# Decay exponents of second chunks from one more masked matmul, with reworked seams between the stages

## The chip, the cores and the metric

The kernel runs on one core of one Trainium2 chip. The metric is the device time of one launch in microseconds (us). The span of a profile runs from the first to the last instruction; the time of an execution is a little longer.

## The reference, cut to what matters

Four layers follow each other on 1024 tokens of width 512 (batch 4, 256 tokens each), each with a residual and a layernorm without weights:

```python
A: x = LN(x + taylor(x) + down(silu(gate(x)) * up(x)))            # hidden 1248
B: x = LN(x + down2(silu(w1'(x)) * w3'(x)))                       # hidden 1376, LoRA added to the weights
C: x = LN(x + out_proj(group_norm(ssd(conv(in_proj(x))) * silu(gate))))   # 128 heads x 64, 8 groups
D: x = LN(x + down3(silu(gate3(x)) * up3(x)))                     # hidden 2048, ternary weights
```

In C, dt is clipped, `cs` is the running sum of `dt * A` inside chunks of 128 tokens, and a sequence of 256 tokens has two chunks. For head h, source token s and target token l, inside one chunk:

```python
Lmat[l, s] = exp(cs[l] - cs[s]) if l >= s else 0
scores = (C[l] . B[s]) * Lmat[l, s]         # cb = C . B is shared by the 16 heads of a group
y[l] = sum_s scores[l, s] * x[s] * dt[s]
```

From the first chunk to the second the factor is exp(cs_second[l] + (cs_end - cs[s])). In D the weights are `sign(w) * (|w| > 0.7 * mean|w|)`, so the mean of |w| over a whole matrix comes first.

## The kernel before, in words

Tokens lie as `x_tokens` (128 partitions x 8 tiles x 512) and, turned, as `xT_hi` and `xT_lo` (a value rounded to fp32r and its rest), in two halves of 512 tokens. Products of such pairs are three matmuls, L70, L71, L72 in `three_products`.

**Stages A, B and D** are `feed_forward`: for each half `hf` a loop over hidden tiles n of 128 (10, 11 and 16 of them). TensorE does `gate_up(n)`, then `down(n-1)`; ScalarE does the SiLU and the rounded part of `hidden`; VectorE does `hidden`, and rounds (A, B) or quantises (D: L406, L410, L427, L430, in `split13` and `split2`) the weights of the tiles to come; GpSimd makes the rests of the weights in A and B and does nothing in D. `Norm` ends a half: sums (L164, or L170 and L172 in D), statistics (L182, L187), square root on ScalarE, L195 scales on VectorE, TensorE turns (L220), ScalarE and VectorE take hi and lo parts (L210, L200). For the first half this is done during the second half's first tiles, in order: in A and B before VectorE's tile 0, with TensorE waiting before `down` of tile 0; in D in tile 1. For the second half it stands at the stage's end. A stage ends with a barrier (`Stage.clear`), and the next stage's first loads are issued behind it.

**Stage C** is `state_space`. A prologue projects B and C of all groups, makes `cb` and the tables of dt and cs, and stores them to DRAM. Then 64 units (two heads each, 128 channels) run in 8 groups of 8, through `for_units`: U counts units, V = U - 1, j = U mod 2. In body(U) TensorE's order is:

```python
in_x(u, 0); squares_sum(u) if u.group_ended; in_x(u, 1)   # 24 matmuls, (16 of one column)
inside(u)                                                 # y of unit V: 32 matmuls
seg(u, 0); seg(u, 1)                                      # exponents of first chunks, h = 0, 1
in_g(u, 0); in_g(u, 1)                                    # 24
out_tile(u, 0..3)                                         # 24, out_proj of the pair before
turn(u, 0); turn(u, 1)                                    # 8 transposes
```

`seg(u, h)` (L1713 on) puts the exponents of *first* chunks of head h, mask included, into bank 6 + h: one bf16 matmul of 512 columns (L1726, identity and mask in the rows below the first 15, sums in those) and one of 56 (L1727). The exponents of *second* chunks come from VectorE: `clamp` (L1245, eight L1255 a unit) takes min(cs_second[l] - cs[s], 0). ScalarE's `decay_exp` does eight L1558 (first to second chunk), two L1563 from the banks, two L1567 over the clamped tiles. VectorE multiplies by `cb` in `decay_round` (L1243, six a unit); `cb` was masked when it was moved (`move_cb`, L1149). ScalarE's order in a unit: `x_tap` (L1437), `x_silu` (L1537), `y_high` (L1510), `decay_exp`, `gate_silu` (L1544), `gate_weights` (L1477), `square` (L1577), `y_high`. GpSimd adds the squares of a group (L1398); at a group's end TensorE's `squares_sum` (L1771) sums them over channels. The group's `rstd` scales its `group_out` into `x_tokens` (L1285).

SP's queue loads weights and rows for a unit in `load_unit`, `load_out`, `load_cs`, `load_rows` (L1087: two small DMAs) and, for a group's first unit, `load_cb`. `store_cb(g)` stores `cb` of a group in the prologue; the one of group 7 stands ahead of the first unit's loads.

Of the kernel before, what the change touches and what calls it, by code (L numbers as in the profile page):

```python
# [10 lines left out]
ALU = mybir.AluOpType  # L11
# [43 lines left out]

D_HIDDEN = 2048
# [18 lines left out]
def for_tiles(eng, tiles, body):  # L75


    body(0, 0)
    body(1, 1)
    pairs = (tiles - 2) // 2 - (0 if tiles % 2 else 1)  # L80
    pairs = pairs - 1 if tiles % 2 else pairs
    with eng.Fori(1, 1 + pairs) as i:
        body(i * 2, 0)
        body(i * 2 + 1, 1)
    for n in range(2 + 2 * pairs, tiles):
        body(n, n % 2)
# [23 lines left out]
class Shared:  # L110


    def __init__(self, nc, ctx, consts_f32):
        self.nc = nc
# [10 lines left out]
class Norm:  # L125

    def __init__(self, sh, ctx, tag, last, from_psum=True):
        nc = sh.nc  # L130
        sem = lambda n: stage_semaphore(nc, ctx, f"{tag}_{n}")
        self.sh, self.last, self.from_psum = sh, last, from_psum
# [3 lines left out]
        self.rstd = ctx.enter_context(nc.sbuf_tensor(f"{tag}_rstd", [P, HT], F32))  # L136
        self.summed = sem("summed")
# [9 lines left out]
    def vector(self, v, hf, out_done=None, scale=None):  # L147
        self.vector_sum(v, hf, out_done, scale)
        self.vector_norm(v, hf)

    def vector_sum(self, v, hf, out_done, scale):


        sh = self.sh
        for t in range(HT):
            x = sh.x[:, HT * hf + t, :]
            if self.from_psum:
                all_done, count, tile_done, before = out_done
                if t < HT - 1:
                    v.wait_ge(tile_done, before + t + 1)  # L160
                else:
                    v.wait_ge(all_done, count)
                if scale is None:
                    v.tensor_tensor(x, sh.bank[t][:, :], x, ALU.add).then_inc(self.summed, 1)  # L164
                else:

                    buf, sc, scaled = scale
                    if t >= 1 or hf:
                        v.wait_ge(self.summed, HT * hf + t)
                    v.tensor_tensor(buf, sh.bank[t][:, :], sc, ALU.mult).then_inc(scaled, 1)  # L170
                    v.wait_ge(scaled, HT * hf + t + 1)
                    v.tensor_tensor(x, buf, x, ALU.add).then_inc(self.summed, 1)  # L172

    def vector_norm(self, v, hf):

        sh = self.sh
        for t in range(HT):
            if self.from_psum:
                v.wait_ge(self.summed, HT * hf + t + 1)
            if hf and t == 0:  # L180
                v.wait_ge(self.stat, 2 * HT)
            v.bn_stats(self.stats[:, t, :], sh.x[:, HT * hf + t, :]).then_inc(self.stat, 1)  # L182
        if hf:
            v.wait_ge(self.normed, HT)
        for t in range(HT):
            v.wait_ge(self.stat, 2 * HT * hf + t + 1)
            v.bn_aggr(self.mv[:, t, :], self.stats[:, t, :]).then_inc(self.stat, 1)  # L187
        v.wait_ge(self.stat, 2 * HT * hf + 2 * HT)
        v.tensor_scalar(self.std[:, :], self.mv[:, :, 1], EPS, None, ALU.add).then_inc(self.var_ready, 1)
        v.wait_ge(self.std_ready, hf + 1)  # L190
        v.reciprocal(self.rstd[:, :], self.std[:, :]).then_inc(self.rstd_ready, 1)
        v.wait_ge(self.rstd_ready, hf + 1)
        for t in range(HT):
            x = sh.x[:, HT * hf + t, :]
            v.tensor_scalar(x, x, self.mv[:, t, 0:1], self.rstd[:, t:t + 1], ALU.subtract, ALU.mult)\  # L195
             .then_inc(self.normed, 1)
        if not self.last:
            for k in range(KT):
                v.wait_ge(self.x_hi, KT * hf + k + 1)
                v.tensor_tensor(sh.xl[:, k, HALF * hf:HALF * (hf + 1)], sh.bank[k][:, :],  # L200
                                f32(sh.xh[:, k, HALF * hf:HALF * (hf + 1)]), ALU.subtract)\
                 .then_inc(self.x_ready, 1)

    def scalar(self, a, hf):
        a.wait_ge(self.var_ready, hf + 1)
        a.activation(self.std[:, :], self.std[:, :], ACT.Sqrt).then_inc(self.std_ready, 1)
        if not self.last:
            for k in range(KT):
                a.wait_ge(self.turned, KT * hf + k + 1)
                a.activation(self.sh.xh[:, k, HALF * hf:HALF * (hf + 1)], self.sh.bank[k][:, :], ACT.Copy)\  # L210
                 .then_inc(self.x_hi, 1)

    def tensor(self, pe, hf):

        if self.last:
            return
        pe.wait_ge(self.normed, HT * (hf + 1))
        for k in range(KT):
            for t in range(HT):
                mm = pe.transpose(self.sh.bank[k][:, P * t:P * (t + 1)],  # L220
                                  self.sh.x[:, HT * hf + t, P * k:P * (k + 1)], self.sh.ident[:, :])
            mm.then_inc(self.turned, 1)


def feed_forward(nc, sh, kind, w13_dram, w2_dram, tiles, extra, out_dram=None):
# [3 lines left out]
    TL = tiles  # L229
    with Stage(nc) as ctx:  # L230
# [6 lines left out]
        norm = Norm(sh, ctx, kind, kind == "D")  # L237

        if kind == "B":
            raw13 = sb("raw13", [P, TL, 2 * D])  # L240
            raw2 = sb("raw2", [P, TL, D])
        else:
            raw13 = sb("raw13", [P, 2, 2 * D])
            raw2 = sb("raw2", [P, 2, D])
        w13h = sb("w13h", [P, 2, 2 * D], F32R)
# [8 lines left out]
        raw13_in = [sem(f"raw13_in{i}") for i in range(2)]  # L254
        raw2_in = [sem(f"raw2_in{i}") for i in range(2)]
        w13_hi, w13_ready = sem("w13_hi"), sem("w13_ready")
# [5 lines left out]
        extra_in = sem("extra_in")  # L262
# [44 lines left out]
        if kind == "D":  # L307
            scales = sb("scales", [P, 2, TL])
            down_scale = sb("down_scale", [P, D])
            ones = sb("ones", [P, P])  # L310
            thr, nthr = sb("thr", [P, 4]), sb("nthr", [P, 4])
            above = sb("above", [P, 2 * D])
            above2 = sb("above2", [P, D])
            scaled_out = sb("scaled_out", [P, D])
            total_mm, thr_done = sem("total_mm"), sem("thr_done")
            above_done, above2_done, scaled = sem("above_done"), sem("above2_done"), sem("scaled")
            ones_set = sem("ones_set")
# [4 lines left out]
        def _(sp):  # L322
# [23 lines left out]
            if kind == "D":  # L346
                sp.dma_start(scales[:, :, :], extra["scales"]).then_inc(extra_in, 16)
                sp.dma_start(down_scale[:, :], extra["down_scale"]).then_inc(extra_in, 16)
            free13 = w13_ready
            free2 = w2_ready  # L350
            for hf in range(2):
                def load(n, par):
                    slot = (hf * TL + par) % 2
                    if hf or not isinstance(n, int) or n >= 2:
# [10 lines left out]
            if kind == "D":  # L365
                for hf in range(2):
                    sp.wait_ge(norm.normed, HT * (hf + 1))
# [21 lines left out]

        @block.vector  # L390
        def _(v):
            scale = (scaled_out[:, :], down_scale[:, :], scaled) if kind == "D" else None
# [57 lines left out]
            def hidden(hf, n, par):  # L450
# [11 lines left out]
                else:  # L462
                    v.tensor_tensor(hid[:, slot, :], up, gated[:, slot, :], ALU.mult).then_inc(hid_done, 1)
                if hf or not isinstance(n, int) or n >= 2:
# [36 lines left out]
            if kind == "D":  # L501
                v.memset(ones[:, :], 1.0).then_inc(ones_set, 1)
                v.wait_ge(total_mm, 1)
                v.tensor_scalar(thr[:, 0:3], sh.bank[0][:, 0:3], 1.0 / (D * D_HIDDEN), THRESHOLD, ALU.mult, ALU.mult)\
                 .then_inc(thr_done, 1)
                v.wait_ge(thr_done, 1)
                v.tensor_scalar(nthr[:, 0:3], thr[:, 0:3], -1.0, None, ALU.mult).then_inc(thr_done, 1)
                v.wait_ge(thr_done, 2)
# [9 lines left out]
            else:  # L518
                split13(0, 0, 0)
# [15 lines left out]
            for hf in range(2):  # L535
# [17 lines left out]
                if hf and kind != "D":  # L553
                    norm.vector(v, 0, (down_mm, TL, rows_done, 0), scale)
                elif hf:
                    norm.vector_sum(v, 0, (down_mm, TL, rows_done, 0), scale)

                def body(n, par):
                    if not (isinstance(n, int) and n + 2 >= TL):
# [8 lines left out]
                    hidden(hf, n, par)  # L568
# [27 lines left out]
                    if kind == "D" and hf and isinstance(n, int) and n == 1:  # L596
                        norm.vector_norm(v, 0)
# [1312 lines left out]
```

## Time and profile before

| | us |
|---|---|
| median of 3 runs | 2311.48 (2309.84 to 2311.51) |
| the profiled execution: time | 2312.29 |
| the profiled execution: span | 2310.5 |
| TensorE busy | 2132.7, mean granted clock 0.958 |
| VectorE busy | 1762.6 |
| ScalarE busy | 1214.7 |
| GpSimd busy | 673.3 |

Stages by the time line: A to 269, B to 517, C's prologue to 649, C's units to 2040, C's end to 2091, D to the end. Busy time of TensorE counts modelled ends of pipelined matmuls; the distance between two starts tells more.

### The profile page before, as it was taken

To read this page: it belongs to the slowest core of one execution; us is meant where nothing else is said; L and a number is where in the kernel's file an instruction comes from. 1 tells how busy PE (TensorE), PEld (TensorE's weight loads), DVE (VectorE), ACT (ScalarE), POOL (GpSimd) and SP (SyncE) were. 2 spreads that over 40 slices of the span, in tenths; PEclk is the share of its full clock that TensorE was granted. 3 is DMA by queue.
4 is the path that set the end of the run, shared out by engine and by line. 5 is a ranking of instruction groups with operands and counts; after the bars stand their busy time and mean duration, and the time that the engine had idled before them with its cause. 6 is when DMAs were issued, how large, how long until landed. Compare 5 with 4: busy or idle time off the path is not lost. (4 is left out here: it accounts for less than half of the span.)

```text
span 2310.5 us, 36141 instructions
## 1 busy us (share of the span) xinstructions
PE 2132.7 (92%) x10769; PEld 1700.1 (74%) x10833; DVE 1762.6 (76%) x2970; ACT 1214.7 (53%) x2182; POOL 673.3 (29%) x406
## 2 busy tenths in 40 slices
PE   7999589988979999999999999999999999967997
PEld 6777478767867777777777777777777777755775
DVE  6434355547868888889889889889889889867887
ACT  2112113334347677667667767767767767732232
POOL 5525044321113324324324324324324324310000
PEclk9999789999989999999999999999999999978998
DMA  4202231213232212212212212212212212103433
GB/s 156 96 28 73 83 133 62 89 47 98 92 106 70 69 60 70 69 60 69 69 60 69 69 60 69 69 60 69 69 60 68 69 61 69 51 0 123 137 109 109
DMA packets 126014, 176.30 MB, mean 76 GB/s; under 512 B 17668, under 2 KB 83716, under 8 KB 125316
## 3 DMA queue, kind: packets, MB, share of 16 engines
q1 hardware_dynamic: 125892, 175.07, 23.8%
q14 instruction: 93, 0.76, 0.1%
q8 instruction: 29, 0.48, 0.1%
HBM read 165.72 MB, written 9.31 MB: 76 GB/s over the span
## 5 line engine op out<-in xcount | busy, mean ns | idle before, releaser
L70 PE MATMUL bank<-xT_hi,C_w_hi 128*128 128x512 f32 x1160 | 478.3, 412 | 14.1 <-POOL C_w_lo L1380 7.5
L72 PE MATMUL bank<-xT_hi,C_w_lo 128*128 128x512 f32 x1160 | 464.9, 401 | 0.0
L71 PE MATMUL bank<-xT_lo,C_w_hi 128*128 128x512 f32 x1160 | 464.6, 401 | 0.0
L1380 POOL TENSOR_TENSOR C_w_lo<-C_raw,C_w_hi 128x512 fp32r<-128x512 f32 x130 | 186.7, 1436 | 736.5 <-ACT C_w_hi L1477 640.3
L1127 DVE SCALAR_TENSOR_TENSOR C_acc<-bank,C_par,C_acc 128x510 f32<-128x510 f32 (+2 forms) x384 | 281.2, 744 | 70.3 <-ACT C_acc L1437 44.8
L1243 DVE TENSOR_TENSOR C_decay<-C_decay,C_cb 128x512 f32<-128x512 f32 x384 | 299.1, 807 | 4.5 <-ACT C_decay L1563 4.5
L70 PEld LDWEIGHTS bank<-xT_hi,C_w_hi 128*128 128x128 f32 x1160 | 222.1, 191 | 70.5 <-POOL C_w_lo L1380 8.8
L72 PEld LDWEIGHTS bank<-xT_hi,C_w_lo 128*128 128x128 f32 x1160 | 221.9, 191 | 54.2
L71 PEld LDWEIGHTS bank<-xT_lo,C_w_hi 128*128 128x128 f32 x1160 | 222.9, 192 | 47.6
L1398 POOL TENSOR_TENSOR C_sq_sum<-C_sq_sum,C_sg 128x1024 f32<-128x1024 f32 x56 | 154.3, 2756 | 212.8 <-DVE C_decay L1243 121.5
L70 PE MATMUL bank<-C_out_hi,C_yg_hi 128*128 128x512 f32 x512 | 202.0, 395 | 7.8 <-DVE C_yg_lo L1213 5.5
L72 PE MATMUL bank<-C_out_hi,C_yg_lo 128*128 128x512 f32 x512 | 201.1, 393 | 0.0
L71 PE MATMUL bank<-C_out_lo,C_yg_hi 128*128 128x512 f32 x512 | 200.0, 391 | 0.0
L1224 DVE TENSOR_TENSOR C_group_out<-bank,C_group_out 128x512 f32<-128x512 f32 x192 | 131.0, 687 | 81.9 <-PE bank L72 81.9
L1437 ACT ACTIVATE C_acc<-bank,C_par_two 128x512 f32<-128x512 f32 x128 | 98.5, 775 | 151.8 <-PE bank L72 144.4
L1706 PE MATMUL bank<-C_decay,C_xd 128*64 128x256 f32 x1024 | 159.2, 390 | 4.3 <-DVE C_decay L1243 4.3
L1558 ACT ACTIVATE C_decay<-C_cs_second,C_end_t 128x128 f32<-128x128 f32 x512 | 157.1, 389 | 0.8
L1537 ACT ACTIVATE C_xs<-C_acc 128x512 f32<-128x512 f32 x128 | 80.5, 629 | 140.6 <-DVE C_acc L1127 140.5
L1510 ACT ACTIVATE C_yg_hi<-C_xs,C_par_two 128x512 fp32r<-128x512 f32 x128 | 92.5, 722 | 90.3 <-DVE C_xs L1208 56.5
L70 PEld LDWEIGHTS bank<-C_out_hi,C_yg_hi 128*128 128x128 f32 x512 | 96.4, 188 | 32.1 <-issue 11.7
L1213 DVE SCALAR_TENSOR_TENSOR C_yg_lo<-C_xs,C_par,C_yg_hi 128x512 fp32r<-128x512 f32 x128 | 113.3, 885 | 3.5 <-ACT C_yg_hi L1510 3.4
L72 PEld LDWEIGHTS bank<-C_out_hi,C_yg_lo 128*128 128x128 f32 x512 | 96.5, 189 | 21.3
(245 smaller groups left out, 4399.3 us busy)
## 6 DMA issues: line engine op xcount, KB each, us to landing
C_raw<-in_Cxg SPq DMA_DIRECT2D x65, 512.0 KB, 3.6
C_cs_second<-cs_rows SPq DMA_DIRECT2D x64, 512.0 KB, 5.0
C_raw_out<-in_Cout SPq DMA_DIRECT2D x64, 256.0 KB, 3.5
D_raw<-in_D SPq DMA_DIRECT2D x32, 512.0 KB, 3.5
A_raw<-in_A SPq DMA_DIRECT2D x20, 512.0 KB, 3.6
B_right_raw<-in_D SPq DMA_DIRECT2D x16, 512.0 KB, 3.7
D_raw<-in_D SPq DMA_DIRECT2D x32, 256.0 KB, 2.6
cb_rows<-C_decay SPq DMA_DIRECT2D x8, 768.0 KB, 3.3
```

What stands on the lines that cost most here:

```text
L70: pe.matmul(out, lh, rh, start=start, stop=False)
L71: pe.matmul(out, lh, rl, start=False, stop=False)
L72: return pe.matmul(out, ll, rh, start=False, stop=stop)
L1127: v.scalar_tensor_tensor(out=sums[:, :, i:], in0=src[:, :].rearrange("p (b t) -> p b t", b=2)[:, :, 0:SEQ - i], scalar=w(TAPS - 1 - i), in ...
L1213: v.scalar_tensor_tensor(out=yg_lo[:, slot, half(h)], in0=xs[:, slot, half(h)], scalar=par_of(V, NORM_W), in1=f32(yg_hi[:, slot, half(h)]) ...
L1224: v.tensor_tensor(group_out[:, t, :], bank[OUT_BANK[k % 4]][:, :], group_out[:, t, :], ALU.add)\
L1243: v.tensor_tensor(e, e, cb[:, r % 2 if r < 4 else 2, :], ALU.mult).then_inc(S.m_done, 1)
L1380: e.tensor_tensor(w_lo[:, slot, :], raw_at, f32(w_hi[:, slot, :]), ALU.subtract).then_inc(lo_done, 1)
L1398: e.tensor_tensor(sq_sum[:, :], sq_sum[:, :], sg[:, 1 - u.j, :], ALU.add).then_inc(S.sq_added, 1)
L1437: a.activation(sums[:, half(h)], src[:, :], ACT.Identity, scale=scale, bias=bias).then_inc(done, 1)
L1558: a.activation(decay[:, 2 * h + b // 2, SEQ * (b % 2) + CHUNK:SEQ * (b % 2 + 1)], cs_second[:, u.j, at:at + CHUNK], ACT.Exp, bias=end_t[:, ...
L1706: pe.matmul(bank[4 + th][q, at:at + SEQ], xd[:, 2 * b, q], decay[:, 2 * h + th, at:at + SEQ], start=True, stop=False)
```

## The change

**In C's units.** `clamp` and its table `cs_t` go, and so do the two L1567 on ScalarE. The sums of both chunks are split into three bf16 parts and stored (`chunk_rows`). `seg(u, c)` now handles chunk c for both heads; `seg(u, 0)` stands where both calls stood, `seg(u, 1)` behind `in_g` and ahead of `out_tile`. Both chunks use banks 6 and 7, so `seg(u, 1)` waits for ScalarE's two exponentials over the first chunks' exponents, and ScalarE's order is `inside_exp(u, 0)`, `across_exp(u)`, `inside_exp(u, 1)`. As masks lie in the matmuls, `move_cb` only copies: 3 operations for 5. `load_rows` has four DMAs for two. In a group's first unit `square` stands ahead of `gate_silu`. In the prologue two of five `dt_turn` go, the parts are made over 1024 columns for 512, and `store_cb(7)` stands behind the first unit's `load_rows`.

**At C's end.** The first two weight tiles of D are loaded, D's threshold is made and its first tile quantised while C's last output tiles run, which get banks of their own. Only the first half of the tokens is normalised there, two of its four scalings on ScalarE; the second half is only summed.

**In A, B and D.** The norm of a half that runs under the next half's tiles is spread over tiles 0 to 3: statistics in tile 0, reciprocal and scaling (all four on ScalarE) in tile 1, the turning in tiles 2 and 3, two blocks each, into the banks of the tile before, with TensorE waiting for the hi and lo parts behind `down`. In D the second half of C's tokens is treated so in the first pass. D's `hidden` stands ahead of its weight work, its rest part is made by GpSimd (`hidden_low`), and so are the residual sums (`half_add`). At a stage's end two of four scalings move to ScalarE. `for_tiles` writes out four first tiles for two.

```diff
-            def seg(u, h):
-                if h == 0:
-                    pe.wait_ge(S.rows_in, u.U * 32 + 32)
...
+            def seg(u, c):
+                if c == 0:
+                    pe.wait_ge(S.rows_in, u.U * 64 + 64)
...
+                for h in range(2):
+                    if c:
+                        pe.wait_ge(S.decays, u.U * EXPS + (h + 1))
+                    elif not u.first:
+                        pe.wait_ge(S.xd_done, u.V * 2 + (h + 1))
+                    pe.matmul(bank[6 + h][:, :], left[:, c, h, :], right[:, c, h, :], start=True, stop=False)
+                    pe.matmul(bank[6 + h][:, :].rearrange("p (b l) -> p b l", b=BATCH)[:, :, 0:REST], left_rest[:, :],
+                              right_rest[:, :, :], start=False, stop=True).then_inc(S.seg_mm, 1)
...
                 seg(u, 0)
-                seg(u, 1)
                 in_g(u, 0)
                 in_g(u, 1)
+                seg(u, 1)
...
-                decay_exp(u)
+                inside_exp(u, 0)
+                across_exp(u)
+                inside_exp(u, 1)
+                if u.group_ends:
+                    square(u)
                 gate_silu(u, 0)
                 gate_silu(u, 1)
...
-                clamp(u, 0)
-                clamp(u, 1)
                 out = not u.first_pair
...
                 load_cs(u)
                 load_rows(u)
+                if u.first:
+                    store_cb(GROUPS - 1)
...
+                    turns = nm is not None and n in (2, 3)
+                    if turns:
+                        pe.wait_ge(hid_done, n + hf * TL)
+                        for k in (2 * n - 4, 2 * n - 3):
+                            nm.turn(pe, k, turn_bank(hf, n, k))
...
                         down(hf, n - 1, 1 - par, isinstance(n, int) and n == 1, False)
+                    if turns:
+                        pe.wait_ge(nm.x_ready, 2 * n - 2)
...
+            def norm_steps(hf, n):        # vector
+                nm = in_pass[hf]
...
+                if n == 0:
+                    for t in range(HT):
+                        nm.stats_of(v, t, nm is not early)
+                    nm.spread(v)
+                elif n == 1:
+                    nm.invert(v)
+                elif n < 4 and not (kind == "D" and hf):
+                    for k in (2 * n - 4, 2 * n - 3):
+                        nm.low(v, k, turn_bank(hf, n, k))
...
+            def norm_steps(hf, n):        # scalar
...
+                if n == 0:
+                    nm.root(a)
+                elif n == 1:
+                    for t in range(HT):
+                        nm.scale_shift(a, t)
+                elif n < 4 and not (kind == "D" and hf):
+                    for k in (2 * n - 4, 2 * n - 3):
+                        nm.high(a, k, turn_bank(hf, n, k))
...
+            first_quantised()             # vector, end of C
+            mean_square(last, GROUPS)
             group_scale(GROUPS)
...
+            for k in range(HT):
+                last_add(k)
+                if k:
+                    norm.stats_of(v, k - 1)
+            norm.stats_of(v, HT - 1)
+            norm.spread(v)
+            norm.invert(v)
+            for t in range(HT // 2):
+                norm.scale(v, t)
+            for k in range(HT, TT):
+                last_add(k)
+            for k in range(KT):
+                norm.low(v, k, bank[TAIL_BANK[k]])
```

## Rows read from the trace of the kernel before

**Rows 1.** The page, section 1: busy us, share of the span, instructions.
```profile
PE 2132.7 (92%) x10769; PEld 1700.1 (74%) x10833; DVE 1762.6 (76%) x2970; ACT 1214.7 (53%) x2182; POOL 673.3 (29%) x406
```

**Rows 2.** Stretches: length, busy us of PE, PEld, DVE, ACT, POOL, clock, DMA.
```profile
1460.00:1480.97 20.97, 20.81 (x118) 16.49 (x117) 17.69 (x32) 15.50 (x28) 6.23 (x4) 1.00 0.09 26
1020.86:1024.27 3.41, 3.41 (x10) 2.64 (x9) 1.97 (x4) 0.00 (x0) 0.00 (x0) 0.50 0.73 249
2120.00:2180.00 60.00, 60.00 (x259) 48.41 (x258) 50.84 (x88) 13.39 (x22) 0.00 (x0) 1.00 0.44 146
```

**Rows 3.** Time line of TensorE, unit 39, around seg: start, length.
```profile
1501.65 0.19 PE L1727 MATMUL bank<-C_right_rest,C_left_rest 128*128 128x56 bf16 x1 [0.16 <-issue]
1501.68 0.38 PE L1726 MATMUL bank<-C_right,C_left 128*128 128x512 bf16 x1
1501.89 0.19 PE L1727 MATMUL bank<-C_right_rest,C_left_rest 128*128 128x56 bf16 x1
1501.92 0.48 PE L70 MATMUL bank<-xT_hi,C_w_hi 128*128 128x512 f32 x1
1502.24 0.39 PE L71 MATMUL bank<-xT_lo,C_w_hi 128*128 128x512 f32 x1
```

**Rows 4.** Groups by line: count, busy and mean, idle before them.
```profile
L1255 DVE TENSOR_SCALAR C_decay<-C_cs_second,C_cs_t 128x128 f32<-128x128 f32 x512 | 106.1, 280 | 2.6 <-DMA C_cs_second<-cs_rows 2.6
L1405 POOL TENSOR_TENSOR x_tokens<-C_group_out,x_tokens 128x512 f32<-128x512 f32 x28 | 35.5, 1301 | 0.0
```

**Rows 5.** Time line, unit 39: ScalarE's exponentials, TensorE's first output matmul.
```profile
1504.33 1.28 ACT L1558 ACT_TABLE_LOAD   x1
1505.63 2.45 ACT L1558 ACTIVATE C_decay<-C_cs_second,C_end_t 128x128 f32<-128x128 f32 x8
1507.60 0.39 PE L70 MATMUL bank<-C_out_hi,C_yg_hi 128*128 128x512 f32 x1
1507.98 1.05 ACT L1563 ACTIVATE C_decay<-bank 128x512 f32<-128x512 f32 x2
```

**Rows 6.** Time line around a group's end, units 16 and 17.
```profile
1006.24 1.28 ACT L1558 ACT_TABLE_LOAD   x1
1007.75 0.49 PE L70 MATMUL bank<-C_out_hi,C_yg_hi 128*128 128x512 f32 x1 [1.11 <-DVE C_yg_lo L1213]
1016.01 2.37 POOL L1398 TENSOR_TENSOR C_sq_sum<-C_sq_sum,C_sg 128x1024 f32<-128x1024 f32 x1 [13.12 <-ACT C_sg L1577]
1016.81 2.12 DVE L1243 TENSOR_TENSOR C_decay<-C_decay,C_cb 128x512 f32<-128x512 f32 x1
1018.51 1.94 PE L1771 MATMUL bank<-C_ones,C_sq_sum 128*128 128x1 f32 x16 [1.35 <-POOL C_sq_sum L1398]
```

**Rows 7.** Time line, unit 19: ScalarE's exp table, TensorE's first output matmul.
```profile
1074.60 1.28 ACT L1558 ACT_TABLE_LOAD   x1
1075.69 0.39 PE L70 MATMUL bank<-C_out_hi,C_yg_hi 128*128 128x512 f32 x1
```

**Rows 8.** Waits of TensorE: us in total, times, longest.
```profile
PE bank L220 <- DVE x_tokens L195: 32.6, 4, 11.0
PE bank L787 <- DVE D_hidl L467: 9.6, 5, 4.7
PE bank L1727 <- DMA C_right<-first_rows: 8.9, 1, 8.9
PE bank L70 <- DVE A_hidl L467: 5.6, 1, 5.6
```

**Rows 9.** Time line, end of C to the start of D.
```profile
2077.93 2.73 DVE L1285 SCALAR_TENSOR_TENSOR x_tokens<-C_group_out,C_rstd,x_tokens 128x512 f32<-128x512 f32 x4
2089.65 1.31 DVE L200 TENSOR_TENSOR xT_lo<-bank,xT_hi 128x512 fp32r<-128x512 f32 x2 [0.16 <-ACT xT_hi L210]
2099.38 0.77 PE L771 MATMUL bank<-xT_hi,D_w13h 128*128 128x512 f32 x1 [6.39 <-DVE D_w13h L410]
```

**Rows 10.** Groups by line of VectorE, 2110 to 2180 us (stage D).
```profile
L467 DVE TENSOR_TENSOR D_hidl<-D_hid,D_hidh 128x512 fp32r<-128x512 f32 x12 | 8.3, 692 | 9.1 <-ACT D_hidh L694 9.1
```

More of the change, by code:

```diff
@@ L75, in for_tiles @@
 def for_tiles(eng, tiles, body):
[L78 to L82, printed above, removed]
+    for n in range(4):
+        body(n, n % 2)
+    pairs = (tiles - 4) // 2 - 1
+    with eng.Fori(2, 2 + pairs) as i:
         body(i * 2, 0)
         body(i * 2 + 1, 1)
-    for n in range(2 + 2 * pairs, tiles):
+    for n in range(4 + 2 * pairs, tiles):
         body(n, n % 2)
@@ L113, in __init__ @@
     def __init__(self, nc, ctx, consts_f32):
[L114 removed]
+        self.nc, self.ctx = nc, ctx
+        self.ahead = None
         self.x = ctx.enter_context(nc.sbuf_tensor("x_tokens", [P, TT, D], F32))
@@ L174, in vector_norm @@
-    def vector_norm(self, v, hf):
-        sh = self.sh
-        for t in range(HT):
[L178 to L222, printed above, removed]
+    def x(self, t):
+        return self.sh.x[:, HT * self.hf + t, :]
@@ L235, in sem @@
             return stage_semaphore(nc, ctx, f"{kind}_{name}")
-        norm = Norm(sh, ctx, kind, kind == "D")
+        norms = [HalfNorm(sh, ctx, f"{kind}{hf}", hf) for hf in range(2)]
+        early = HalfNorm(sh, ctx, f"{kind}_in", 1) if kind == "D" else None
+        in_pass = (early, norms[0])
         if kind == "B":
@@ L746, in body @@
                              .then_inc(term_hi, 1)
-                    if kind == "D" and hf and isinstance(n, int) and n == 1:
-                        norm.scalar(a, 0)
-                if hf and kind != "D":
-                    norm.scalar(a, 0)
+                    norm_steps(hf, n)
                 for_tiles(a, TL, body)
-            norm.scalar(a, 1)
+            norms[1].root(a)
+            for t in range(HT // 2, HT):
+                norms[1].scale_shift(a, t)
+            if kind != "D":
+                for k in range(KT):
+                    norms[1].high(a, k, sh.bank[k])
         @block.tensor
@@ L881, in _ @@
                 down(hf, TL - 1, (TL - 1) % 2, False, True)
-            norm.tensor(pe, 1)
+            if kind != "D":
+                for k in range(KT):
+                    norms[1].turn(pe, k, sh.bank[k])
 PAR = 8
@@ L979, in state_space @@
         rstd = sb("rstd", [P, TT])
-        raw_bc = sb("raw_bc", [P, 2, BC])
+        raw_bc = ahead.first
         consts_raw = sb("consts_raw", [P, P + HALF])
@@ L1376, in _ @@
+            for k in range(KT):
+                norm.low(v, k, bank[TAIL_BANK[k]])
         @block.gpsimd
@@ L1617, in _ @@
             root(GROUPS)
-            for hf in range(2):
-                norm.scalar(a, hf)
+            group_scaled(last, GROUPS)
+            norm.root(a)
+            for t in range(HT // 2, HT):
+                norm.scale_shift(a, t)
+            for k in range(KT):
+                norm.high(a, k, bank[TAIL_BANK[k]])
         @block.tensor
@@ L1793, in _ @@
             inside(last)
-            for k in range(TT):
-                out_tile(last, k)
-            squares_sum(last)
-            pe.wait_ge(S.ms_done, GROUPS)
-            for hf in range(2):
-                if hf:
-                    pe.wait_ge(norm.x_ready, KT)
-                norm.tensor(pe, hf)
+            pe.wait_ge(S.g_silu, last.U * 2)
+            pe.matmul(bank[3][:, 0:3], ahead.ones[:, :], sh.abs_totals[:, :], start=True, stop=True).then_inc(S.total_mm, 1)
+            out_tile(last, 0)
+            out_tile(last, 1)
+            squares_sum(last)
+            for k in range(2, TT):
+                out_tile(last, k)
+            for k in range(KT):
+                norm.turn(pe, k, bank[TAIL_BANK[k]])
 DT_V = 10
```

431 lines of the change are left out of this document (260 added, 171 removed).

## The prediction

> **What bounds the kernel now.** I read the page first: TensorE is busy 92% of the span, VectorE 76% [rows 1]. Then the stretches. A regular unit of stage C takes 20.97 us, and TensorE is busy in 20.81 of them at full clock, VectorE in 17.69, ScalarE in 15.50 [rows 2]. Sixty-four units are 1,370 of the 2,310 us, so what counts there is TensorE's order alone: every matmul added to it is paid, and work taken from VectorE is worth nothing by itself. D's loop is the same: 60.00 of 60 us [rows 2]. Third, the waits of TensorE [rows 8] and the time lines around them: its idle time lies at the seams, at the turn from one half of the tokens to the other, and once a group. Behind such idle time the clock falls to its lower level: in the 3.41 us behind a group's end it was 0.50, so a fall costs 1.7 us beside the idle time [rows 2, 6]. The sum below is made against the profiled execution, 2312.3 us (span 2310.5); the median is 2311.5, so 0.8 comes off at the end.
>
> **1. The second seg, every unit.** Two matmuls of 512 columns and two of 56 join TensorE's order. From one L1727 to the next, over one L1726, are 0.24 us, so four take 0.48; the first L70 behind them lasts 0.32 to the next start where 0.23 is usual, 0.09 more [rows 3]. That is 0.57 us. Before the first L1727 the trace also shows 0.16 us of "issue"; it comes after `inside`, whose last matmuls are short, and I don't expect it behind `in_g`. Bounds 0.48 to 0.73; 64 x 0.57 = **+36 us** (31 to 47). No other work hides it, TensorE is full. The removed `clamp`, 106.1 us of VectorE [rows 4], and the L1567 return nothing: VectorE waits for the output matmuls next anyway.
>
> **2. A new wait in TensorE's order.** `seg(u, 1)` waits for ScalarE's exponentials over the first chunks, since banks 6 and 7 are theirs; behind it stand the output matmuls and all that follows. In unit 39 the table is loaded by 1505.6 and two exponentials take 1.05, to 1506.7; TensorE is through with `in_g` at 1507.6: 0.9 us to spare [rows 5]. Units with j = 0 have a margin 1.0 shorter, so some 0.4 for the first head, none for the second. In a group's first unit the table is there at 1007.5, the exponentials end 1008.1 and 1008.6, while `in_g` ended 1.11 + before 1007.75 [rows 6]: output begins at about 1009.0 instead of 1007.75, 0.7 beyond the 0.57. In the units behind a group's end ScalarE is late by `root` and `group_scaled`: in unit 19 its exponentials could end at 1076.4, TensorE wants them at 1075.7 [rows 7]. I add 0.7 + 0.6 + 0.2 + 0.3 us for the first four units of a group, each stall giving the next unit slack: 1.8 x 7 = **+12 us**. Below: nothing but the first, 4. Above: if ScalarE's chain follows TensorE in all j = 0 units, 0.5 more each, 25.
>
> **3. A group's end.** The sum of squares kept TensorE waiting 1.35 us at 1018.5 [rows 6]. ScalarE's `square` moves ahead of a table load, two SiLUs and a copy (1.28 + 1.1 + 0.6): GpSimd begins some 3 us earlier relative to ScalarE, and the wait goes: 7 x 1.3 = **-9 us**. What becomes late next is VectorE: the GpSimd addition now falls on `decay_round`, which waits behind it as at 1016.81 (2.12 us for one) [rows 6]; the next unit needs its products 5 us later, so this is hidden. The sixteen one-column matmuls, 1.9 us, stay, so the clock may still fall. I take half of 7 x 1.7: **-6 us** (0 to -12).
>
> **4. C's start.** The rows of the first unit stood behind `store_cb(7)` in SP's queue and TensorE waited 8.9 us [rows 8]. Now they go ahead. What is late next is `move_cb(7)`, three copies behind the last `cb` matmul, about 2.3 us. 8.9 - 2.3, and less time at the lower clock, but second `seg` needs exponentials that wait for the store: **-7 us** (-3 to -11). The prologue's fewer transposes (-1) and longer parts on VectorE (+1) cancel.
>
> **5. From C to D.** Before, the last sum of the second half starts at 2077.93, its norm and turning end at 2090.96, and D's first matmul is at 2099.38 behind a barrier, a load and the quantising [rows 9]. After: output tiles end at 2062 as before; `group_add`, `last_add` and statistics of the first half until 2065.9, scaled by 2068, turned and split by 2073; barrier 1.5; D starts at **2074.5**, 24.9 earlier. But the second half's norm is now in D's first tiles. VectorE has statistics (3 us) in tile 0; ScalarE waits for them with the root, loads tables twice (1.28 each) and has the SiLU of tile 1 behind it; so tile 1's `hidden` comes at +16 us, the reciprocal at +22, four scalings to +24.4, while TensorE wants to turn at +14.8. Then `low` stands behind `split2(n+1)`, which waits for the very `down(n-1)` that precedes TensorE's wait: 2.5 and 3.6 us more. With 5 us at the lower clock tile 4 starts at about +44, where +23 was usual. 24.9 - 21.5: **-3 us** (-20 if the steps fit under the matmuls, +6).
>
> **6. The half turns of A and B.** The waits of 5.6 us [rows 8] and 3.4 at the lower clock go. In their place: 2.6 for the scalings (again behind the root and its tables), and twice about 2 for `split2` and two `low` behind `down`. With the clock: **0** (-9 to +7 for both). Ends of A and B: two of four scalings beside the others, 0.5 each: **-1**.
>
> **7. D.** Its half turn cost waits of 2.7, 0.8 and 4.7 (of the 9.6 in [rows 8]) and two falls. Spread out, statistics and both table loads still stand between tile 0 and the `hidden` of tile 1: about 8 us and one fall: **-4** (-10 to +2). The end: GpSimd adds while VectorE multiplies, -2.1, and `hidl` 0.6 longer: **-1.5**. The loop: VectorE has 50.84 us in 60 [rows 2], 10.8 tiles of 24 matmuls, 4.7 a tile of 5.56. `hidl` (0.69 [rows 10]) goes to GpSimd (1.30 [rows 4]): **+1** (0 to +10).
>
> The memory rule behind that last bound: the Trainium skill, "SBUF — State Buffer", section "Who interferes with whom", says that GpSimd and a VectorE instruction with two SBUF inputs exclude each other for a whole instruction. By that rule the trace agrees at 1016.81 [rows 6].
>
> A rule that speaks against moving roots into tile 0: the Trainium skill, "ScalarE: Activation LUTs", section "What ACT_TABLE_LOAD costs", gives 2.66 us for a switch, a drain of 1.38 included. The row says otherwise: the load starts 1504.33, takes 1.28, and the exponential starts 1505.63 [rows 5]. By the page the three half turns and D's start would each be 2.8 us worse; I go by the row.
>
> **Sum.** 36 + 12 - 9 - 6 - 7 - 3 + 0 - 1 - 4 - 1.5 + 1 = +17.5. 2312.3 + 17.5 - 0.8 = **2329 us**.
>
> **Rivals.**
> - *TensorE paced by ScalarE* (10 in 100): the new wait bites in all j = 0 units. Part 2 at 25 instead of 12, clock falls at each group's end stay, +6: 2348. For it: the margin of 0.4. Against it: TensorE's unit grows by 0.57, and ScalarE's by nothing.
> - *The seams fit* (other side, 22 in 100): the spread norm costs TensorE only the structural waits of some 2 us, because scaling ends before tile 2's `gate_up`. Then part 5 gives -20, part 6 -8, part 7 another -6: 31 less, 2298; from 22 less on the kernel is faster. For it: VectorE is idle for about half of each tile in A and B. Against it: the in-order queue of ScalarE, where SiLU(1) stands behind the root.
> - *Half of that* (10 in 100): 18 less, 2311, no change.
> - *D held by VectorE* (8 in 100): each GpSimd `hidl` blocks VectorE for 1.30 us; 4.7 - 0.69 + 1.30 = 5.3 is still under 5.56, but GpSimd's own instruction stretches to 1.7 when both meet, and VectorE's waits with it: 5.9, +0.35 x 28 tiles = +10: 2339. The page on SBUF named above is the general form of this.
> - *The change doesn't do what it says*: the second `seg` costs nothing, since its operands are bf16 and short. Only if TensorE had gaps; 20.81 of 20.97 excludes it. None.
> - The forecast, 50 in 100; its own range 2316 to 2342.
>
> **Chances and range.** A measurement can't tell less than 0.2%, 4.6 us, from no change. Faster: the fitting seams, 22, less a few where parts 1 and 2 are at their tops: 0.20. Same: 0.13. Slower: 0.67. The bounds of the loop (35 to 72) and the seams (-41 to +10) don't fall together; I keep 2300 to 2347, which leaves the best seams and the worst pacing out.
>
> **What would show it.** Regular unit 21.5 us in the stretches, with L1726 128 more times; a wait of TensorE for ScalarE's L1563 successor before some seg; no wait of L1771 for GpSimd; D's first matmul some 25 us before its old place relative to C's last output tile; in tiles 1 to 3 behind each turn, waits of transposes for ScalarE's scalings and of gate_up for VectorE's `low`. It is wrong if the unit grows by over 0.9 or under 0.4, or if those waits are absent.

## The result, and the profile after

The changed kernel takes 2348.7 us (median of 4 runs, 2348.6 to 2351.2) against 2311.5 (2309.8 to 2314.8): ratio 1.0164, 95% interval 1.0151 to 1.0176, 37 us slower. The forecast was 2329: the direction came, at twice the size, and the time lies 1.7 us above the range.

First the changed kernel's page and stretches. The columns are those of [rows 2]: length, then busy us of PE, PEld, DVE, ACT, POOL, granted clock and DMA.

```profile
PE 2161.6 (92%) x11017; PEld 1710.1 (73%) x11081; DVE 1700.0 (72%) x2383; ACT 1226.8 (52%) x2207; POOL 741.8 (32%) x450
...
1482.00:1503.50 21.50, 21.34 (x121) 16.70 (x121) 16.79 (x25) 15.40 (x28) 5.81 (x4) 1.00 0.17 50
...
1032.70:1035.70 3.00, 3.00 (x14) 2.13 (x13) 2.85 (x6) 0.00 (x0) 0.00 (x0) 1.00 0.95 302
166.80:173.70 6.90, 5.71 (x18) 4.89 (x19) 1.98 (x2) 3.12 (x6) 6.74 (x6) 0.51 0.24 97
...
2117.08:2175.44 58.36, 42.39 (x152) 33.38 (x153) 35.55 (x59) 16.72 (x24) 9.10 (x5) 0.78 0.23 78
```

A regular unit now takes 21.50 us. The 3.00 us behind the sum of squares at a group's end run at clock 1.00, where the same work ran at 0.50 before [rows 2]. A's half turn (166.8) runs at 0.51, the lower of the two levels (1.2 GHz). The last row is D's start, from its first `gate_up` to that of the seventh tile (five whole tiles and the sixth's `gate_up`), called D's first five tiles below: 58.4 us with TensorE busy in 42.4. Here is the same work before:

```profile
2099.38:2133.68 34.30, 33.53 (x137) 26.72 (x138) 27.85 (x49) 8.16 (x12) 0.00 (x0) 0.95 0.42 132
```

TensorE's waits after: total, times, longest, to be read beside [rows 8]. L1853 and L1854 are `seg`, L1830 is `inside`, L192 the turning, L72 and L851 the matmuls that need `xT_lo` (`low`, L201), L867 `down`.

```profile
PE bank L192 <- ACT x_tokens L186: 34.4, 6, 9.4
...
PE bank L1853 <- ACT C_decay L1671: 15.4, 14, 1.4
PE bank L1830 <- issue: 13.0, 7, 1.9
...
PE bank L72 <- DVE xT_lo L201: 9.2, 4, 3.0
...
PE bank L867 <- POOL D_hidl L654: 8.4, 4, 5.1
...
PE bank L851 <- DVE xT_lo L201: 6.6, 2, 4.0
```

The waits for the sum of squares (8.9 before) and for the first unit's rows (8.9) are gone. New are `seg`'s (forecast), seven of 1.86 us ahead of `inside` (not forecast; the profile names no releaser, "issue"), and those for `low`.

The two time lines, laid over each other by the starts of TensorE's matmuls, say where the 36.6 us of span came from. The middle column is the forecast for the same stretch, from its own terms.

| stretch | forecast | measured |
|---|---|---|
| A and B, to C's first matmul (521.90, now 529.03) | -1 | +7.1 |
| C's prologue, to the first unit | 0 | +1.0 |
| first unit, to its first turning | -6 | -5.3 |
| units, first turning to last (1358.75, now 1398.95) | +32 | +40.2 |
| last turning to D's first matmul (64.53, now 39.26) | -24.9 | -25.3 |
| D (211.12, now 230.02) | +17.4 | +18.9 |

Four of the six rows fit to 1.5 us or better. The miss is in A and B (8 us) and in the units (8 us). In the units, 63 steps from one to the next grew by 0.52 each, 33 us; the first step grew 2 us beyond that (its cause was not followed up) and the groups' ends 5.

The time line around a group's end, unit 17, TensorE and then VectorE (start, length; in brackets the idle time before):

```profile
1020.99 0.39 PE L1853 MATMUL bank<-C_right,C_left 128*128 128x512 bf16 x1 [1.43 <-ACT C_decay L1671]
...
1035.31 0.39 PE L74 MATMUL bank<-xT_hi,C_w_lo 128*128 128x512 f32 x1
1037.56 0.65 PE L1830 MATMUL bank<-C_decay,C_xd 128*64 128x256 f32 x4 [1.86 <-issue]
```

```profile
1025.99 2.88 DVE L1332 TENSOR_TENSOR C_decay<-C_decay,C_cb 128x512 f32<-128x512 f32 x1
...
1034.76 2.51 DVE L1221 SCALAR_TENSOR_TENSOR C_acc<-bank,C_par,C_acc 128x510 f32<-128x510 f32 x3
1037.19 0.16 DVE L1346 TENSOR_SCALAR C_ms<-bank 128x8 f32<-128x8 f32 x1
```

`inside` starts 0.2 us after L1346, `mean_square`, has ended. That operation reads the sums out of bank 4, which `inside` overwrites, and stands behind three convolutions in VectorE's order. The wait's cause can be read from this coincidence, but only the runs below show it.

D's second and third tile, ScalarE, then what TensorE and VectorE do at their end:

```profile
2125.06 1.28 ACT L168 ACT_TABLE_LOAD   x1
2131.62 0.21 ACT L168 ACTIVATE D_in_std<-D_in_std 128x4 f32<-128x4 f32 x1 [5.27 <-DVE D_in_std L164]
2131.84 1.28 ACT L749 ACT_TABLE_LOAD   x1
2133.14 0.69 ACT L749 ACTIVATE D_gated<-bank,ahead_scales 128x512 f32<-128x512 f32 x1
...
2139.23 2.92 ACT L186 ACTIVATE x_tokens<-x_tokens,D_in_shift,D_in_rstd 128x512 f32<-128x512 f32 x4 [3.96 <-DVE D_in_shift L174]
```

```profile
2147.77 0.75 DVE L471 SCALAR_TENSOR_TENSOR D_w2h<-ahead_raw,ahead_nthr,D_above 128x512 fp32r<-128x512 f32 x1
2148.44 1.28 DVE L201 TENSOR_TENSOR xT_lo<-bank,xT_hi 128x512 fp32r<-128x512 f32 x2
```

ScalarE waits 5.27 us for the statistics with the SiLU of the next tile behind the root; the scalings end at 2142.15 and TensorE, which had waited 9.37 us for them, turns at 2142.30. At the end of the tile `low` (L201) runs behind `split2` (L471), and the next `gate_up` starts at 2149.78, 0.06 after it.

### The profile page after: what moved, and what is told of

It is laid out like the page before. It is cut to its first block and busy times, and to the rows that moved or that the text cites. A ratio compares the mean times of both kernels' runs of the same rounds, so it can differ in the third digit from the quotient of the medians.

```text
span 2347.1 us, 35872 instructions
## 1 busy us (share of the span) xinstructions
PE 2161.6 (92%) x11017; PEld 1710.1 (73%) x11081; DVE 1700.0 (72%) x2383; ACT 1226.8 (52%) x2207; POOL 741.8 (32%) x450
## 5 line engine op out<-in xcount | busy, mean ns | idle before, releaser
L72 PE MATMUL bank<-xT_hi,C_w_hi 128*128 128x512 f32 x1160 | 473.3, 408 | 16.2 <-POOL C_w_lo L1493 9.0
L73 PE MATMUL bank<-xT_lo,C_w_hi 128*128 128x512 f32 x1160 | 459.8, 396 | 0.0
L74 PE MATMUL bank<-xT_hi,C_w_lo 128*128 128x512 f32 x1160 | 459.7, 396 | 0.0
L1493 POOL TENSOR_TENSOR C_w_lo<-C_raw,C_w_hi 128x512 fp32r<-128x512 f32 x130 | 180.1, 1385 | 717.3 <-ACT C_w_hi L1591 639.7
L1332 DVE TENSOR_TENSOR C_decay<-C_decay,C_cb 128x512 f32<-128x512 f32 x384 | 336.6, 904 | 8.9 <-ACT C_decay L1680 8.9
L72 PEld LDWEIGHTS bank<-xT_hi,C_w_hi 128*128 128x128 f32 x1160 | 220.3, 190 | 70.4 <-POOL C_w_lo L1493 10.3
L1313 DVE TENSOR_TENSOR C_group_out<-bank,C_group_out 128x512 f32<-128x512 f32 x184 | 126.1, 685 | 177.3 <-PE bank L74 177.3
L72 PE MATMUL bank<-C_out_hi,C_yg_hi 128*128 128x512 f32 x512 | 205.4, 401 | 2.0 <-issue 2.0
L1830 PE MATMUL bank<-C_decay,C_xd 128*64 128x256 f32 x1024 | 159.7, 389 | 17.3 <-issue 13.0
L1671 ACT ACTIVATE C_decay<-bank 128x512 f32<-128x512 f32 x256 | 137.6, 590 | 0.7
L1302 DVE SCALAR_TENSOR_TENSOR C_yg_lo<-C_xs,C_par,C_yg_hi 128x512 fp32r<-128x512 f32 x128 | 121.6, 950 | 5.4 <-issue 3.1
L72 PEld LDWEIGHTS bank<-C_out_hi,C_yg_hi 128*128 128x128 f32 x512 | 96.5, 188 | 27.6 <-issue 2.0
```

The lines of the kernel that those rows point to most:

```text
L72: pe.matmul(out, lh, rh, start=start, stop=False)
L73: pe.matmul(out, lh, rl, start=False, stop=False)
L74: return pe.matmul(out, ll, rh, start=False, stop=stop)
L1302: v.scalar_tensor_tensor(out=yg_lo[:, slot, half(h)], in0=xs[:, slot, half(h)], scalar=par_of(V, NORM_W), in1=f32(yg_hi[:, slot, half(h)]) ...
L1313: v.tensor_tensor(group_out[:, t, :], bank[OUT_BANK[k % 4]][:, :], group_out[:, t, :], ALU.add)\
L1332: v.tensor_tensor(e, e, cb[:, r % 2 if r < 4 else 2, :], ALU.mult).then_inc(S.m_done, 1)
```

## Experiments

Twelve kernels. Ratios are to the kernel before, run on the same chip, with 95% intervals; "from the change" is the difference to 2348.7.

**1. The old loop in the changed seams.**

```diff
-                seg(u, 0); in_g(u, 0); in_g(u, 1); seg(u, 1)      # TensorE, per unit
+                seg(u, 0); seg(u, 1); in_g(u, 0); in_g(u, 1)      # one chunk, head h
+                clamp(u, 0); clamp(u, 1)                          # VectorE, and masks in move_cb again
```

> The changed kernel with the loop over the units as before: one seg, the clamps on VectorE, the mask in the cb products. All seams stay changed. Reading of the changed trace: a regular unit went from 20.98 to 21.50 us, 64 x 0.52 = 33.7, and at a group's end the second seg waits 1.43 + 0.90 us for ScalarE where 1.11 was waited before, 7 x 1.2 = 8.5; so 2348.7 - 42 = 2306. Rival, that the waits are there in any case and only move: 2348.7 - 33.7 = 2315. Rival, that the changed seams gain nothing and the loop costs all of the difference: 2311.

Measured: 2307.1 us, 0.9975 (0.9966 to 0.9985), 41.6 below the change. So the loop costs 42 us and all the changed seams together are worth 5. A regular unit is 20.93 us here and 21.51 in the changed kernel, 0.58 for the loop alone. The wait at `inside` is there in this kernel too (15.1 us in seven times): it belongs to the seam, not to the second `seg`. Four of the seven are 2.4 us long, and behind three of these four the clock fell; those groups' second units take 26.6 to 26.9 us where three of the others take 24.6. The first of the three falls:

```profile
1199.95:1203.36 3.41, 3.41 (x24) 2.64 (x20) 2.52 (x4) 2.23 (x4) 0.00 (x0) 0.50 0.00 0
```

**2. `mean_square` ahead of the convolutions.**

```diff
+                if u.group_ended:
+                    mean_square(u, g)
                 for h in range(2):
                     ... tap, three conv ...
-                    if u.group_ended and h == 0:
-                        mean_square(u, g)
```

> The changed kernel with VectorE's mean_square ahead of the first half's convolutions in a group's second unit. If the 1.86 us before inside (seven times, called issue) are the wait for mean_square behind three convolutions, they go: 2348.7 - 13 = 2336. Rival: inside waits as long for the masked decays or the scaled x, which VectorE also makes late there: 2348. Rival: the wait goes, but the next unit's second seg waits longer for ScalarE, whose root is behind the same mean_square: half, 2342.

Measured: 2333.6 us, 1.0091 (1.0074 to 1.0108), 15.1 below. The wait of L1830 for "issue" is gone from the list, a group's second unit falls from 25.24 to 23.34 us in all seven groups (13.3 in sum), and the next unit's 22.8 stays. It was `mean_square`.

**3. A's and B's half turn as before.**

```diff
-        in_pass = (early, norms[0])
+        in_pass = (early, norms[0] if kind == "D" else None)
+        # VectorE, ahead of the second pass: stats, spread, invert, scale x4, low x4
+        # TensorE, ahead of the first down: turn x4
```

> The changed kernel with the half turns of A and B in one go as before (all four scalings on VectorE ahead of the second pass, the turning before the first down). By the stretches of the two traces A's turn took 57.8 us where 51.2 were before, B's 51.3 where 48.5 were: 2348.7 - 9.4 = 2339. Rival, the forecast's part 6, that the turns cost the same and A and B are longer for another reason (their ends): 2348.

Measured: 2338.8 us, 1.0114 (1.0097 to 1.0131), 9.9 below. C's first matmul comes 10.0 us earlier than in the changed kernel, so the half turns carry the whole difference of A and B (7.1).

**4. The second `seg` between the output tiles.**

```diff
-                seg(u, 1)
                 for k in range(HT):
+                    if k == 2:
+                        seg(u, 1)
                     out_tile(u, k)
```

> The changed kernel with the second seg between the second and the third output tile instead of ahead of the first. If the wait of TensorE for ScalarE's first exponentials is all that the place costs, the units with excess (1.83 and 1.30 us beyond a regular unit in each group) fall to the 0.75 that the output matmuls wait for yg_lo anyway: 7 x (1.1 + 1.3) = 17, 2332. Rival, that what TensorE gains there it gives back at inside behind a group's end, since VectorE's chain and its mean_square don't come earlier: 7 x 1.3 = 9, 2340. Rival, that the exponentials over the second chunks, now 2.8 us later, hold the turning of x: 64 x 0.3 slower, 2360 and over.

Measured: 2337.9 us, 1.0114 (1.0097 to 1.0131), 10.9 below, between the first two. But for 0.5 us in the very first pair, `seg` doesn't wait for ScalarE any more; a group's first unit falls from 23.33 to 22.38 and its third from 22.82 to 21.53, but the second, with the wait at `inside`, goes from 25.24 to 25.39, and to 27.1 in the two groups where the clock falls behind it. Part of the gain is given back there.

```profile
PE bank L1830 <- issue: 13.9, 7, 2.0
```

The third theory is out: the exponentials over the second chunks, 2.8 us later, hold nothing; a regular unit is 21.53.

**5. The norm's steps one tile later** (root in tile 1, scalings in 2, turning in 3 and 4).

```diff
-        STATS, ROOT, INVERT, SCALE, TURN = 0, 0, 1, 1, 2
+        STATS, ROOT, INVERT, SCALE, TURN = 0, 1, 2, 2, 3      # `for_tiles` writes out six first tiles for four
```

> The changed kernel with the steps of the spread norm one tile later in A, B and D: root behind hidden of tile 1, reciprocal and scalings at the end of tile 2, turning in tiles 3 and 4. If what costs is that root stands ahead of the SiLU of tile 1 in ScalarE's order while VectorE's statistics are not there, TensorE's waits of 10.9 us in A, 6.7 in B and 16 in D and their clock falls go in large part: -6, -5 and -20, 2318. Rival, that the steps cost their own time on ScalarE and VectorE wherever they stand: the waits move by a tile and the time stays, 2347.

Measured: 2333.7 us, 1.0092 (1.0075 to 1.0108), 15.0 below, half of the first theory. TensorE's waits for scalings fall from 34.4 to 21.5 us, and those for `low` stay (9.4 + 7.6 where 9.2 + 6.6 were). So the place of the steps is one cause of two. That it is the root ahead of the SiLU is read from the time line above and not shown by itself: this run moves the root, the scalings and the turning together.

**6. `low` ahead of `split2`.**

```diff
+                    norm_lows(hf, n)                  # tiles 2 and 3 behind a turn
                     split2(hf, n + 1, 1 - par)
                     ...
-                    for k in (2 * n - 4, 2 * n - 3):  # was at the tile's end
-                        nm.low(v, k, turn_bank(hf, n, k))
```

> The changed kernel with the two low of tiles 2 and 3 behind a turn ahead of split2 in VectorE's order, where they wait for the turning only and not for the down that follows it. The waits of gate_up for low are 3.03 + 2.06 us in A, 1.79 + 2.35 in B and 2.62 + 3.98 in D, 15.8 in all, and part of the lower clock is behind them. If the order on VectorE causes them: 2348.7 - 14 - 3 = 2332. Rival, that ScalarE's high is what is late (behind silu and hidden of the same tile): two thirds stay, 2344.

Measured: 2332.9 us, 1.0097 (1.0080 to 1.0114), 15.8 below. The waits for `low` fall by 6.4 us only:

```profile
PE bank L72 <- DVE xT_lo L201: 5.7, 3, 2.3
...
PE bank L855 <- DVE xT_lo L201: 3.7, 2, 2.8
```

By the starts of `gate_up`, though, A's turn is 7.0 us shorter, B's 3.3 and D's first five tiles 7.8, 18 in sum. The rest goes with time at the lower clock: 129 us of the profile are at the lower level where 160 were. Both theories had a part: what remains is `high` and `low` one after the other, what went was `split2` and the clock behind it.

**7. All of it together.** The edits of runs 1, 2, 5 and 6 in one kernel.

> The loop as before, mean_square ahead of the convolutions, the norm's steps one tile later, and low ahead of split2, in one kernel. If the parts add up: 2348.7 - 41.6 (old loop) - 15.1 (mean_square) - 15.0 (steps later) - 17 (low first) = 2260. Rival, that they overlap, since with the old loop the waits of a group's end were partly for GpSimd's sum and the low waits are fewer when the steps are later: 2275. Against the kernel before: 0.978 to 0.985.

Measured: 2261.5 us, 0.9784 (0.9767 to 0.9800). The parts add up to 87.5, and 87.3 came. This agreement is in part luck, for by stretches they don't add up: the units, first turning to last, are 57.9 us shorter where the four runs' own differences make 50.8 (run 1 still had the wait at `inside` and its three falls), and all the rest of the span is 30 us shorter where they make 42, as runs 5 and 6 shorten the same turns.

**8. Both halves normalised at C's end.**

```diff
-        early = HalfNorm(sh, ctx, f"{kind}_in", 1) if kind == "D" else None
+        early = None
+            norm2 ... stats, spread, invert, scale, turn, high, low behind norm's, at C's end
```

> The changed kernel with the norm of the second half of tokens at C's end, behind that of the first, instead of in D's first tiles. The norm in D's tiles costs 58.4 us over five tiles where 34.3 were before, 24.1 more; at C's end it should cost a root, scalings, transposes, high and low behind the first half's, 9 to 13 us. So 2348.7 - 24 + 11 = 2336. Rival, that most of the stretch in D's first tiles is the lower clock and the first tile's own start and stays: 2352.

Measured: 2333.5 us, 1.0099 (1.0082 to 1.0116), 15.3 below. D's first five tiles are regular again, 25.1 us less, with D starting 9.3 us later behind C's last unit:

```profile
2125.23:2158.48 33.25, 33.25 (x137) 26.61 (x138) 29.82 (x45) 9.21 (x13) 9.16 (x5) 0.95 0.42 138
```

**9 and 10. The best seams, with the old loop and with the changed one.** Run 9 adds the edit of run 8 to run 7. Run 10 has run 9's seams, the changed loop and run 4's place for the second `seg`.

> The kernel with the old loop, mean_square first, steps one tile later and low first, and the norm of both halves at C's end, so that D's first tiles are regular. In that kernel D's first five tiles take 49.8 us; with both norms at C's end they took 33.2, and C's end grew by 8.2: 2261.5 - 16.6 + 8.2 = 2253, against the kernel before 0.975. Rival, that the gain at D's start and the better order there are the same gain, 2260.

> The same seams with the changed loop (second seg, between the second and third output tile). If what the second seg costs is its own matmuls alone once its wait is gone: 34 above its sister with the old loop, 2287. Rival, that its waits at a group's end stay as well: 42 above, 2295.

Measured: 2255.0 us, 0.9755 (0.9739 to 0.9771), 6.4 less than run 7 of the 8.4 expected, and 2283.4 us, 0.9883 (0.9866 to 0.9900). With its waits gone the changed loop costs 28.4 us, less than both theories. Regular units differ by 0.60 us (21.53 and 20.93), 38 in all, and a group's first and third unit give some of it back: the output matmuls' wait for `C_yg_lo` is 1.0 us there where run 9 has 9.8. That this is because `clamp` is no longer in VectorE's way was not tested.

**11 and 12. The kernel before with `square` moved, and with `mean_square` moved too.**

```diff
                 decay_exp(u)
+                if u.group_ends:
+                    square(u)
                 gate_silu(u, 0)
```

> The kernel before with one edit: in a group's first unit square stands right behind the exponentials in ScalarE's order. By part 3 of the forecast the wait for the sum of squares goes and the clock falls half as often: 2311.5 - 15 = 2296. By the changed trace TensorE then waits for mean_square at inside, 1.86 us of the 1.35 + 1.7 gained: 7 x 1.2 = 8 or, as the group's period in the changed seams with the old loop says (173.8 us where it was 173.9), next to nothing: 2304 to 2311.

> The kernel before with square moved as in the run beside it, and mean_square ahead of the first half's convolutions. If mean_square behind three convolutions is what took the gain back, the whole of it comes out here: 7 x 2.9 = 20, 2291. Rival, that inside then waits for the masked decays instead: 2304 or above.

Measured: 2310.5 us, 1.0000 (0.9991 to 1.0010), and 2295.4 us, 0.9932 (0.9915 to 0.9948). The move alone can't be told from nothing (the units of its trace are 4.3 us shorter); with `mean_square` out of the convolutions' way it is worth 17 us by the medians, and 15.9 in the units of the trace. `mean_square` moved alone in this kernel was not run. Run 11's time line, TensorE and VectorE:

```profile
1022.43 0.39 PE L72 MATMUL bank<-xT_hi,C_w_lo 128*128 128x512 f32 x1
1024.52 0.65 PE L1709 MATMUL bank<-C_decay,C_xd 128*64 128x256 f32 x4 [1.71 <-issue]
```

```profile
1021.73 2.51 DVE L1127 SCALAR_TENSOR_TENSOR C_acc<-bank,C_par,C_acc 128x510 f32<-128x510 f32 x3
1024.15 0.16 DVE L1271 TENSOR_SCALAR C_ms<-bank 128x8 f32<-128x8 f32 x1
```

`inside` again starts when `mean_square` is through (1024.31). In this kernel nothing else of the change is present, so the step is isolated.

## Why the prediction was wrong, step by step

**Part 1, the second seg: right.** 0.52 us a unit for 0.57, 33.5 for 36, and against run 1, which differs in the loop alone, 0.58. That nothing of VectorE's relief comes back held for regular units; at a group's end run 10 gets some 1.4 us back each, which may be that relief.

**Part 2, the wait for ScalarE: right in size and nearly in place.** The forecast spread it over a group's first four units; it came in two. The 15.4 us are 1.43 in a group's first unit (six times), 0.90 in its third (seven) and 0.50 in the very first; 0.23 between the heads comes to 3 more, and the 5.5 us that the output matmuls waited for `C_yg_lo` (one is in [rows 6]) went in exchange. Net 13 for 12; run 4 gave 10.9 for undoing it. The rival, TensorE paced by ScalarE in all units with j = 0, is out: 14 waits in 64 units. The measured time is the 2348 of that rival by coincidence only.

**Part 3, a group's end: the first step that failed.** "What becomes late next is VectorE [...] the next unit needs its products 5 us later, so this is hidden." I asked after the products and not after `mean_square`, which is also VectorE's and which `inside` waits for. Before, it ended at 1023.11 and `inside` started at 1024.83; with the 0.2 us from the one to the other it had 1.5 us in hand. TensorE became earlier by 1.35 of wait and 1.6 of lower clock, VectorE later by 0.3 (6.2 us from the end of the first `in_x` to that of `mean_square`, where 5.9 were): 2.95 + 0.3 - 1.5 = 1.75, and 1.86 is the wait. VectorE and TensorE before:

```profile
1018.85 1.75 DVE L1213 SCALAR_TENSOR_TENSOR C_yg_lo<-C_xs,C_par,C_yg_hi 128x512 fp32r<-128x512 f32 x1
...
1022.96 0.15 DVE L1271 TENSOR_SCALAR C_ms<-bank 128x8 f32<-128x8 f32 x1
1024.83 0.65 PE L1706 MATMUL bank<-C_decay,C_xd 128*64 128x256 f32 x4
```

The -9 came, and the -6 came as 7 x 1.6 = -11 (none of the seven falls at a group's end is left), but 13.0 us of new wait took them back: -7 for the -15. Run 2 removed it in the changed kernel. In the one before run 11 brought it about and run 12 removed it, and there the whole of part 3 came: 15.9 us in the units for the 15 of the forecast. What made VectorE 0.3 us later was not taken apart. GpSimd's sum now runs from 1025.82 to 1028.32 and `decay_round` beside it takes 2.88 us for one, where before there were two such holds, 2.12 [rows 6] and the 1.75 above; over the whole kernel the mean of `decay_round` went from 807 to 904 ns. With the rule of the Trainium skill that the prediction draws on ("SBUF — State Buffer", "Who interferes with whom"), that the two engines exclude each other, the trace agrees: the 2.88 us end 0.55 behind GpSimd's sum.

**Part 4: right** (-5.8 for -7, the second seg taken out); the prologue took 1 us more.

**Part 5: right.** D starts 25.3 us earlier (24.9) and its first five tiles give back 24.1 (21.5), net -1.2 for -3. The seams rival (-20) was wrong in this form, but its target exists: run 8 gets 15 us with another order.

**Part 6, the half turns of A and B: the second step that failed.** "In their place: 2.6 for the scalings [...] and twice about 2 [...] With the clock: 0." In A the wait for the scalings was 5.8, those for `low` 3.0 and 2.1; in B 2.5, 1.8 and 2.4. So among the waits the term that was mis-sized is A's scalings (5.8 for 2.6); most of the rest is the clock. A's turn took 57.8 us over four tiles for 51.2, B's 51.3 for 48.5: +9.4, less 2.3 at starts and ends. I had priced the root and its tables, but not that the reciprocal stands behind a `split2`, which in A took 2.59 us beside GpSimd's 2.82 at 160.42 (time lines below; it takes 0.41 where GpSimd stands still). The `shift` behind it took 1.24, again beside GpSimd, where B has 0.16. Together that is 3.3 us, and A's wait exceeds B's by 3.2. And I had the lower clock go where it stayed: in A, [rows 8]'s one wait of 5.6 became three, each with its stretch at 0.5. Run 3 (9.9 for undoing) shows the size, runs 5 and 6 the two causes: the place of the steps (root ahead of SiLU among them) and VectorE's order (`low` behind `split2`, which waits for the `down` that TensorE runs first). The forecast named both and took them too low.

```profile
160.42 2.82 POOL L676 TENSOR_TENSOR A_w13l<-A_raw,A_w13h 128x1024 fp32r<-128x1024 f32 x1
160.93 2.59 DVE L474 TENSOR_SCALAR A_w2h<-A_raw 128x512 fp32r<-128x512 f32 x1
163.44 0.16 DVE L172 RECIPROCAL A_rstd<-A_std 128x4 f32<-128x4 f32 x1
163.64 1.24 DVE L174 SCALAR_TENSOR_TENSOR A_shift<-A_mean_var,A_rstd 128x4 f32<-128x4 f32 x1
```

**Part 7: right.** Turn -3.1 (-4), end -1.3 (-1.5); a regular tile 5.55 for 5.59, so `hidl` on GpSimd cost nothing, and the rival of D held by VectorE is out.

**The range.** It ended at 2347 because the bounds "don't fall together". The two failures of 8 us each took 2329 to 2345; the other four rows of the table, 2.8 us in sum, and 0.6 between the profiled executions and the medians took it over the bound. The seven-fold term for a group's end had a bound for a gain kept and one for a gain halved, but none for a gain taken back by the wait behind it.

**The table load.** The prediction set the Trainium skill's price ("ScalarE: Activation LUTs", "What ACT_TABLE_LOAD costs"), with a drain of 1.38 us, against the row. The trace doesn't agree with the page: after the change the load starts at 1019.04, 0.02 behind the end of the instruction ahead of it, and the exponentials at 1020.34, again 1.30 later. The measurement decides.

## What to carry to other kernels

Before a stall is counted as gained, list every semaphore that the next waiting instruction holds, and for each the margin by which it was early: here 2.95 us a group were won at one wait, the next semaphore had 1.5 in hand, and 1.86 came back as a new wait. A norm spread over tiles was dear where a step stood ahead of what another engine's next tile waits for; moved by one place (`low` ahead of `split2`) or one tile, the same work cost 15 us less. And edits that each look neutral can hide a large sum: the seams as written were worth 5 us, with three orders mended and one norm moved back 57 (run 9 against the kernel before).

## What the runs showed of the hardware

TensorE's clock at a group's end: before, 0.90 to 1.35 us idle and sixteen one-column matmuls were followed by 3.4 us at 0.50 in all seven groups. With the sum of squares on time the same sixteen matmuls were followed by full clock in all seven, and 1.86 us of idle time 5 us later, behind the second `in_x`, brought no fall either. In run 4 all seven of those later waits are 1.99 us, and two had a fall behind them; in run 11 two are 2.4 us, and none had one; in run 1 four are 2.4 us, and three had one. So what a group's end costs in clock could not be told from the length of one wait.

A VectorE instruction with a single SBUF input was also slow beside GpSimd: the `split2` of 2.59 us above, beside GpSimd's L676. In A the fourteen L474 that met no GpSimd instruction took 0.41 to 0.43 us, the six that met one 1.26 to 2.59. The forecast had looked for this only at instructions with two.
